# A gated attention and mixture-of-experts layer: maxima transposed in fp32 with the shifts read from PSUM, the first half's expert choice and 18 scatters inside the attention, weights scaled on ScalarE

## What is computed

```python
x = x + tanh(g_xattn) * attention(layernorm(x), ctx, ctx, mask)     # 16 heads of 8 features, 128 keys
x = x + tanh(g_ffn) * ffn(layernorm(x))
# ffn, for every token t:
shared = mean over 2 shared experts of gelu(x @ sW1 + sb1) @ sW2 + sb2       # 128 -> 512 -> 128
gates  = x @ rW + rb ; the two best of 8 experts, softmax over these two
moe    = sum over the two chosen of prob * (gelu(x @ W1[e] + b1[e]) @ W2[e] + b2[e])
```

## Time and profile before

| what | value |
|---|---|
| three runs | 524.61, 524.55 and 527.96 us, median 524.61 |
| span of the profiled execution | 524.9 us |
| attention, from the first exponential to the last body | 52.6 to 248 us |
| shared experts | 248 to 361 us |
| routed experts | 361 to 510 us |
| final sum and stores | to 524.9 us |
| instructions | 13531 |

### The profile page before, as it was taken

How to read it: one execution, slowest core, us unless ns; L and a number is a source line. 1 busy time by engine, 2 the same in 40 slices (tenths; PEclk the granted TensorE clock), 3 DMA queues, 4 the chain that set the end, 5 groups by cost and what they waited for, 6 DMA issues and landing times.

```text
span 524.9 us, 13531 instructions
## 1 busy us (share of the span) xinstructions
PE 415.9 (79%) x4611; PEld 297.2 (57%) x4611; DVE 397.8 (76%) x983; ACT 340.8 (65%) x674; POOL 315.9 (60%) x382
## 2 busy tenths in 40 slices
PE   0377979879998989776784989898999989998930
PEld 0245767758776877554341433344878777776720
DVE  7696769868778778987774896494888768886795
ACT  0536857657787877665663876495677567765743
POOL 9151524494987889598876376650466656666550
PEclk9998989899999999988997989999999999999985
DMA  8767863442333534540011011113122222244119
GB/s 226 223 197 202 223 146 80 103 101 75 78 87 84 114 82 142 178 164 17 26 51 45 27 41 41 47 36 81 36 78 77 70 72 86 67 132 138 58 44 280
DMA packets 71753, 53.19 MB, mean 101 GB/s; under 512 B 7473, under 2 KB 63548, under 8 KB 71688
## 3 DMA queue, kind: packets, MB, share of 16 engines
q1 hardware_dynamic: 64608, 42.96, 30.2%
q0 software_dynamic: 4544, 8.44, 4.6%
q10 hardware_dynamic: 2536, 0.94, 0.7%
HBM read 29.38 MB, written 24.33 MB: 102 GB/s over the span
## 4 chain that ended last, share of the span: by engine, by line
PE 25%; DVE 8%; issue 5%; another core or an unknown queue 5%; ACT 4%; POOL 2%; DMA 1%; ACTq 0%; DVEq 0%; POOLq 0%
PE pAtt L1123 9%; PE pE L1111 4%; PE pS L1111 4%; DVE HH L1490 3%; PE pAtt L1061 2%; PE pMix L1101 2%; PE pS L999 2%; ACT H L767 1%; POOL yd L622 1%; PE pE L999 1%; DVE HH L1486 1%; ACT G L803 1%; DMA YY<-yd 1%; DVE t_X L1543 1%
## 5 line engine op out<-in xcount | busy, mean ns | idle before, releaser
L622 POOL DMA_INDIRECT yd<-Y,XR x78 | 85.0, 1089 | 72.5 <-DVE Y L1529 45.4
L1234 DVE TENSOR_REDUCE t_MX<-pS 128x4 f32<-128x512 f32 x128 | 86.4, 682 | 24.0 <-PE pS L861 22.4
L720 ACT ACTIVATE PT<-pE,t_mbias,t_scl 128x512 f32<-128x512 f32 x128 | 97.1, 788 | 6.6 <-PE pE L861 6.4
L597 POOL DMA_INDIRECT xs<-t_STG,t_pos x64 | 64.2, 1002 | 36.5 <-issue 15.4
L1123 PE MATMUL pAtt<-t_W2h,HR 128*128 x624 | 65.3, 219 | 6.8 <-issue 5.5
L803 ACT ACTIVATE G<-pS,t_b1T,t_inv 128x256 f32<-128x256 f32 x78 | 40.0, 569 | 43.6 <-remote 39.3
L1490 DVE SCALAR_TENSOR_TENSOR HH<-H,t_sc,HH 128x512 f16<-128x512 f32 x64 | 48.4, 761 | 21.6 <-ACT HH L772 14.7
L1521 DVE SCALAR_TENSOR_TENSOR HR<-G,t_sc,HR 128x512 f16<-128x512 f32 x78 | 58.6, 751 | 2.8
L1123 PE MATMUL pAtt<-t_W2l,HR 128*128 x312 | 56.4, 219 | 3.4 <-issue 3.4
L1123 PEld LDWEIGHTS pAtt<-t_W2h,HR 128*128 128x128 f16 x624 | 50.0, 97 | 12.6 <-issue 10.9
L861 PE MATMUL pE<-t_Q,t_K 128*128 128x128 f16 x512 | 51.6, 225 | 5.8 <-DMA t_Q<-MPT 4.8
(11 more groups left out here) (276 smaller groups left out, 1044.5 us busy)
## 6 DMA issues: line engine op xcount, KB each, us to landing
xs<-t_padrow SPq DMA_DIRECT2D x10, 516.0 KB, 5.3
XR<-xs SPq DMA_DIRECT2D x39, 129.0 KB
scr<-QKS SPq DMA_DIRECT2D x16, 256.0 KB, 2.2
t_Q<-scr SPq DMA_DIRECT2D x16, 256.0 KB
t_K<-scr SPq DMA_DIRECT2D x32, 128.0 KB
t_STG<-in_W SPq DMA_DIRECT2D x7, 512.0 KB, 6.4
YY<-yd SPq DMA_DIRECT2D x14, 256.0 KB, 5.8
t_X<-in_x SPq DMA_DIRECT2D x4, 512.0 KB, 6.5
```

What stands on the lines that cost most here:

```text
L597: g.indirect_dma_start(k.xs, bass.IndirectOffsetOnAxis(ap=pos[:, n:n + 1], axis=0), k.PAY[:, n, :], None).then_inc(h.di[q], 16)
L622: g.indirect_dma_start(k.yd, bass.IndirectOffsetOnAxis(ap=XR[u][:, q, D:ROW], axis=0), Y[u][:, q, :], None, bounds_check=2 * T - 1, oob_is ...
L720: act.activation(PT[:, m % NPT], pE[g % 2][:], ACT.Exp, bias=k.mbias[:, bt:bt + 1], scale=k.scl[:, bt:bt + 1]).then_inc(s.exp, 1)
L1234: v.tensor_reduce(out=MX[:, n % G // 4, m % 2, m // 2::2], in_=pS[n % 2][:], axis=AX_X, op=ALU.max).then_inc(s.max, 1)
```

## The change

1. **Shifts.** PE transposes the fp32 maxima themselves, in step 3 of the body as before, into two slots of `pAtt1` (16 rows of 2 x 128), and waits for the maxima and for DVE's last reading of those slots. ACT copies them scaled by -1/32768 to fp16 (the high part), and DVE, one step later, forms the low part from PSUM and the high part. L1240 to L1243 are gone. SP sends the two parts with two DMAs in place of one; the second waits for DVE. `MX` is double buffered. PE's values of the second sequence wait for DVE's low part, since they overwrite the slots. The constants of the key and query tiles change to fit.
2. **Weights.** ACT scales each piece in place (`scale_weights`, in steps 2 and 5); POOL is left with cast and subtract and waits for ACT. The pieces come one in body 5, two in each of bodies 6 to 14, one in body 15; DVE's first scales move from step 5 to step 1 of body 5.
3. **Rows and choice.** Pairs 0 to 7 are normalised for bodies 7 to 14 in place of 9 to 16, with four `RSTD` turns for them in place of two. DVE's generator for the first half starts in body 14, step 5; PE's `prefixes(0)` moves to body 15, step 5, into `pMix`, and DVE copies the sums out of PSUM.
4. **Scatters.** 18 of the first half's 32 go into bodies 16 to 19 (2, 5, 5, 6), each time ahead of the payloads of that body; the payloads of `LAST` come behind them, then the other 14, with a pace 22 behind `h.lo` in place of 8. The second half's wait for `h.lo` at two less than before. The index write is split in two.
5. **Padding.** One of SP's ten padding DMAs in each of bodies 5 to 14.

```diff
-    SPLIT = LAG + 3
-    FIRST_W2 = 4
-    UBODIES = END - SPLIT - 1
+    SPLIT = LAG + 2
+    split_done = lambda which, e: SPLITS.index((which, e)) + 1
+    FIRST_ROWS = NP // 2 - 1
+    SCATTERED = {16: 2, 17: 5, 18: 5, 19: 6}
+    PACED = 4
+    SECOND_FROM = 22
-    shifts16 = pM[0:4 * HD, 0, :].bitcast(F16)
+    shifts = pA[1][0:2 * HD, 0:2, :]
-    pR, pC = ([in_part(t[:, q, :]) for t in (pS[0], pM)] for q in range(2))
+    pR, pC = ([in_part(pM[:, slot + q, :]) for slot in (2, 0)] for q in range(2))
     def units_of(t):
-        at = lambda j: min(max(j, 0) * UNITS // UBODIES, UNITS)
+        at = lambda j: min(max(2 * j - 1, 0), UNITS)
     def normalised_in(t):
-        if not 9 <= t < END:
-            return ()
-        return (t - 9,) if t <= 16 else (2 * t - 26, 2 * t - 25)
+        if FIRST_ROWS <= t < FIRST_ROWS + NP // 2:
+            return (t - FIRST_ROWS,)
+        return (2 * t - 26, 2 * t - 25) if NP < t < END else ()
-    RSTD = {8: (0, 4), 12: (4, 4), 16: (8, 4), 18: (12, 2), 20: (14, 2)}
+    RSTD = {6: (0, 2), 8: (2, 2), 10: (4, 2), 12: (6, 2), 16: (8, 4), 18: (12, 2), 20: (14, 2)}
# SP
-                    sp.wait_ge(s.t2, t - 1)
-                    sp.dma_start(k.Q[v][SHIFT:SHIFT + 4, :, :], MPT[t % 2][:]...).then_inc(s.m[v], 16)
+                    for n, done in ((0, s.t2), (1, s.mp)):
+                        sp.wait_ge(done, t - 1)
+                        sp.dma_start(k.Q[v][SHIFT + n:SHIFT + 4:2, :, :], MPT[t % 2][n]...).then_inc(s.m[v], 16)
-                for n in {15: range(0, 3), 16: range(3, 6), 17: range(6, NE)}.get(t, ()):
-                    padding(n)
+                if LAG + 2 <= t < LAG + 2 + NE:
+                    padding(t - LAG - 2)
# POOL, split_weights
-                g.tensor_scalar(stg, stg, k.sc[:, sc:sc + 1], None, ALU.mult).then_inc(s.wh, 1)
-                g.wait_ge(s.wh, 2 * n + 1)
+                g.wait_ge(s.ws1, n + 1)
# POOL, body, behind split_weights and ahead of the payloads
+                if t == NP - 1:
+                    first_index(0)
+                    g.wait_ge(k.s_empty, 16 * NE)
+                for _ in range(SCATTERED.get(t, 0)):
+                    next(scattered)
# POOL, behind the bodies
+            for p in LAST:
+                payload(p)
+            for _ in scattered:
+                pass
+            first_index(1)
+            for _ in scatter_part(1, -SECOND_FROM):
+                pass
# ACT
+            def scale_weights(n):
+                which, e = SPLITS[n]
+                act.wait_ge(s.ws, which + 1)
...
+                act.activation(stg, stg, ACT.Copy, scale=k.sc[:, sc:sc + 1]).then_inc(s.ws1, 1)
-                act.activation(MPT[t % 2][:]..., shifts16, ACT.Copy).then_inc(s.t2, 1)
+                act.activation(MPT[t % 2][0], shifts, ACT.Copy, scale=-1.0 / BIG16).then_inc(s.t2, 1)
+                    if g in (2, 5) and g // 3 < len(units_of(t)):
+                        scale_weights(units_of(t)[g // 3])
# PE
+                    if bb == 1:
+                        pe.wait_ge(s.mp, min(pair + 2, NP))
             def transpose_shifts(t, a):
-                pe.wait_ge(s.mp, t - 1)
-                if a:
-                    pe.wait_ge(s.vev, t + 1)
+                pe.wait_ge(s.max, G * (t - 1))
+                wait(pe, s.at, 2 * (t - LAG))
                 for bb in range(2):
-                    ins = pe.transpose(shifts16[...], MP[:, bb]..., k.ident16[:])
+                    ins = pe.transpose(shifts[:, bb, :], MX[:, t % 2, bb]..., k.identf[:])
-                    if t == END - 2 and g == 1:
+                    if t == NP - 1 and g == 5:
                         prefixes(0)
# DVE
-                link(v.tensor_scalar(NM[:], MX[:], -SCORE_TOP, -1.0 / BIG16, ALU.max, ALU.mult))
-                wait(v, s.nmT, n - 1)
-                link(v.tensor_copy(MP[:, :, :, 0, :], NM[:]))
-                v.tensor_tensor(MP[:, :, :, 1, :], NM[:], MP[:, :, :, 0, :], ALU.subtract).then_inc(s.mp, 1)
+                hi, lo = MPT[t % 2]
+                v.wait_ge(s.t2, t - 1)
+                v.scalar_tensor_tensor(out=lo, in0=shifts, scalar=-1.0 / BIG16, in1=hi, op0=ALU.mult, op1=ALU.subtract).then_inc(s.mp, 1)
-                    if g == PH and b:
-                        less_maxima(t - 2)
                     maximum(G * (t - 1) + g - PH)
+                    if b and g == (PH if t < LAG else PH + 1):
+                        less_maxima(t)
+                link(v.tensor_copy(G2[:], pR[0]))
+                settle(v, l.seen)
-                    if t == LAG + 2 and g == 5:
+                    if t == LAG + 2 and g == 1:
                         first_scales()
-                    if t == END - 3 and g < G - 1:
+                    if t == NP - 2 and g > 4 or t == NP - 1 and g != 4 or t >= NP:
                         next(first, None)
-                    if t == END - 2 and g > 1 or t == END - 1:
-                        next(first, None)
+                    if t >= NP:
                         next(first, None)
```

More of the change, by code:

```diff
@@ L603, in second_index, with scatter_part @@
                        channel_multiplier=NT).then_inc(l.idx, 1)
-                g.wait_ge(l.idx, TABLES + q + 2)
-            first_index()
-            g.wait_ge(k.s_empty, 16 * NE)
-            for part in range(2):
+                g.wait_ge(l.idx, TABLES + 3 * (q // 2) + q % 2 + 2)
+            def scatter_part(part, after):
                 g.wait_ge(l.slots, part + 1)
-                scatter(0, 2 * part)
-                if part == 0:
-                    for p in LAST:
-                        payload(p)
-                scatter(0, 2 * part + 1)
+                for q in (2 * part, 2 * part + 1):
+                    yield from scatter(0, q, after)
                 for q in (2 * part, 2 * part + 1):
                     second_index(q)
-                    scatter(1, q)
+                    yield from scatter(1, q, after)
+            scattered = scatter_part(0, sum(SCATTERED.values()) + PACED)
+            turns(body)
+            for p in LAST:
[5 more added lines that the diff above has]
+                pass
             for i in range(NTILE):
```

102 lines of the change are left out of this document (56 added, 46 removed).

## The result

The changed kernel takes 543.57 us (median of four runs, 543.04 to 545.41), the kernel before 526.29 on the same chip: ratio 1.033, interval 1.0289 to 1.0371. It is slower by 17 us, outside the predicted range of 513 to 534. The profiled executions span 541.3 and 524.9 us.

| stretch | before | after | difference | predicted |
|---|---|---|---|---|
| start to body 8 | 121.43 | 119.36 | -2.1 | 0 |
| bodies 8 to 13 | 69.41 | 72.58 | +3.2 | +2.0 |
| bodies 14 to 16 | 34.67 | 42.82 | +8.2 | +1.3 |
| body 17 to the first gelu | 23.73 | 31.51 | +7.8 | -1.0 |
| first gelu to the third output of the shared stage | 51.41 | 43.45 | -8.0 | -5.5 |

A forecast was written before the change was run, and what follows sets the result against it. PE was taken to set the pace in bodies 8 to 13, DVE in the three after; terms 0 + 2.0 + 1.3 - 1.0 - 2.0 - 0.5 = -0.2 us on 524.9 gave 524.7, median 524.4, range 513 to 534.

The forecast's parts named there:

- rival 3: Attention: runs of five or six scatters hold PE's releases, 3.3 us each, three runs cost 10 us: 534; chance 0.11.
- -0.5 us for the shared stage: Behind the bodies: the first half's shorter scatter run, -3.5, and the second half's longer late stretches, +3; range -8 to +6.
- Bodies 3 to 7, 0: 52.57 to 121.43 us: later low-part DMA (+1.4) and DVE's moved scales (up to -2) can be absorbed; -2 to +3.
- Bodies 8 to 13, +2.0: Six bodies: ACT's second scaling and POOL's payload chain into an 11.9 us cycle, 71.4 against 69.4 us.
- Bodies 14 to 16, +1.3: Three bodies: DVE's work with choice and slots moved in is 36.0 us in a stretch of 34.67; -4 to +3.
- Tail, -1.0: Last bodies: scatters replace weight pieces on POOL, rows come earlier, DVE's late work takes some back; -4.5 to +1.
- Payloads of the last pairs, -2.0: Behind the bodies: payloads no longer wait for eight scatters, so PE's 1.99 us wait goes; 0 to -2.3.
- Scatters of the first half, -3.5: Shared stage: 14 scatters left make a run of 18 us where one of 25 stood, shortening the lateness by 3.5 us.
- Second half, +3: Shared stage: scatters run two further before pausing, so two late stretches can each be 1.3 to 2.6 us longer.
- rival 2: Shared stage: faster by scatters alone, first late stretch vanishes, second ones do not grow: -8, 516; chance 0.11.
- The rule of the Trainium skill: Tail: GpSimd and VectorE share a port lock, so scatters beside DVE would stretch, putting -1.0 nearer its upper end.
- My sign for the lateness: Attention: remote waits between 215 and 250 us would show the prediction wrong.

## Why the prediction was wrong

**The step that failed** is the one under rival 3: "Against: the first eight scatters, ahead of the payloads, have no remote wait beside them." I had read the lateness in the shared and the routed stage right in the main, gave it a term of -0.5 us for the shared stage and none in the sums for bodies 14 to 16 (+1.3) and the tail (-1.0), and let those eight scatters speak against it in the attention, at a chance of 0.11. The two sums came out at +8.2 and +7.8. The 18 scatters cost the attention 18.5 us, where the rival had three runs at 3.3 us.

What the eight could say was less than I took from it. Beside the first three, PE's releases do arrive: L929 ends at 247.07 and DVE takes it up at 247.10, L951 ends at 247.19 and ACT takes it up at 247.65. Behind that ACT is busy and comes to each result of PE only some 1.5 us after it is there (a chunk of L999 is done at 251.56, ACT's gelu of it starts at 253.13), so a release that is late by up to that would leave no wait. In bodies 17 to 19 of the changed kernel ACT and DVE take PE's results as they come. The rows of the kernel before beside the third of the eight scatters:

```profile
247.10 0.35 DVE L1256 SCALAR_TENSOR_TENSOR t_X<-pOut,t_gt,t_X 128x128 f32<-128x128 f32 x1 [1.12 <-PE pOut L929]
```

```profile
247.65 0.27 ACT L692 ACTIVATE t_G<-pMix,t_inv 128x16 f32<-128x16 f32 x1 [0.82 <-PE pMix L951]
```

Even so the eight are not fully explained: in the changed kernel L962's release at 229.92 is late when only two scatters have ended.

The 3.3 us were priced from the routed stage, where they stand behind runs of four, and I put them on runs of five and six. That half clock follows the gaps adds to it (windows four and five: 0.79 and 0.68); how much, no run shows.

Point by point:
- **Bodies 3 to 7, 0**: they ended 2.1 us sooner, but that was this execution. The nine profiled kernels whose bodies 3 to 7 are those of the changed one reach body 8's mark between 119.4 and 124.1 us, at 122.5 in the median; three whose bodies are those of the kernel before at 119.2 to 121.4, the six with shifts alone on the same chips at 117.5 to 120.2, in the median 118.6. By the medians that is +3, the upper end of what I gave: the shifts gain about 1 us here, and the rest of the change costs some 4.
- **Bodies 8 to 13, +2.0**: +3.2 measured. The chain was the right one: PE's weight loads wait for the payload (3.2 us in 6 places, half of the 1 us a body that I named) and POOL up to 3.2 us for ACT's second scaling; the cycle was 12.1 for 11.9, and moving the scaling breaks it. What the sum missed is the alternative. It compared with a kernel whose shifts were slow; with fast shifts alone the cycle is 11.2, so scaling and early rows cost 5.4 us, not 2 to 3, and the 67.11 us with the scaling moved say that all of it is the place of the second scaling.
- **Bodies 14 to 16, +1.3**: +8.2. Without the scatters they take 37.1 us, +2.4, so 5.8 us come with the scatters, all in body 16, and 1.1 us are left. For these I hold it against my sum that over three bodies it lets one body lend time to another. DVE's work was below the 36.0 I had counted (32.7 busy), but 12.8 of it fell in body 15, and PE waits 4.3 us there for maxima, in five places: what is full is one body, not the stretch.
- **Tail, -1.0**: +7.8. Without the scatters it was 18.8 us, -4.9, 0.4 beyond the good end of the range I gave for it with them (-4.5).
- **Payloads of the last pairs, -2.0**: right, no wait. **Scatters of the first half, -3.5**: right in sign; the two together gave -8.0 for the forecast -5.5. **Second half, +3**: right in kind, +7.2. I had priced two scatters. With the number set back the stretch takes 62.1 us, so 5.2 of the 7.2 hang on it; that longer runs delay the split count, and so lengthen the next run, is my reading of it.
- **Half right in the rivals**: the shared stage's time went as rival 2 said for its first part, and against it for the second.
- The rule of the Trainium skill weighed there (SBUF — State Buffer, Who interferes with whom) would have made the scatters longer. They took 0.997 us in the mean, 1.002 before: POOL was not held up, others were. One of the rows that I set against the rule was misread: L1280's 1.02 us (234.49 to 235.51) stand beside POOL's subtraction L537 (234.32 to 235.49), not beside its scaling.
- My sign for the lateness, remote waits between 215 and 250 us, came: DVE's 4.61, ACT's 4.30 and 3.63.

What stays open: what in the chip delays the releases; why one chip shows none of it, and by how much the change is slower or faster there, since the changed kernel was not run on it; the 6.8 us that split runs still cost; and what a pause would give in the routed stage, where runs of four leave ACT 39 us of waits. None was put there.

## What to carry to other kernels

Waits with an unnamed releaser that end, again and again, about when another engine pauses are to be taken as a mechanism and tested: before moving that engine's work, look at who needs a release within the next microseconds at the new place. An observation "there is no wait beside it" counts only where somebody would have waited. Try to break rows of indirect DMAs with a pause (here about a microsecond behind every fourth, in the attention and the shared stage), but first find the slack of their list; and measure on more than one chip, because such a cost can be the chip's. When an engine is filled up, sum its work by the smallest piece in which others wait for it, not by the stage.

## What the runs showed of the hardware

On three of four chips, releases of PE came late beside an unbroken run of scatters. Many arrived 0.4 us before to 2.5 us behind its end, some in its middle (10.77 us of wait ended 10.4 us before the run of 27 did). The longest remote wait of ACT beside the first half's run in the shared stage was 2.1 to 4.5 us with 14 scatters, 4.5 and 5.9 with 19, 13.5 with 20, 8.7 with 22, 19.8 with 25 and 10.8 with 27; with a pause behind every eighth 6.3, behind every fourth none. In the routed stage runs of four left 3.3 us each. It depends on what else waits, so this is a direction and not a law. PE's own matmuls drip in such a run, with idle times of 0.2 to 1 us between groups that wait for nothing (the rows of L932 above). On the fourth chip a run of 66 scatters left no such wait.

The same program on two chips differs by 25 us in its span (511.3 and 486.1) with nearly the same durations of its instructions: a scatter of the routed stage takes 1.08 and 1.12 us. The page Perfetto Trace Analysis of the Trainium skill (Summary: the profiler window per engine type) says that for TensorE the propagation of a semaphore update lies outside what the profiler reports, and that the end it reports is an estimate. The trace fits: L946's row ends at 230.61, PE works on at 231.10, the reader starts at 234.76, and no row holds the time between; on which part of the way it is lost, no run shows. The Trainium skill's page SBUF — State Buffer (Who interferes with whom) says that PE and ACT never wait on anyone; as to the ports no run here speaks against it, but in the time they do wait, beside POOL's scatters.
